# First attention's scores from rounded halves of q and k, both heads side by side in three products

## The reference

```
q = jnp.einsum('ahe,bce->bach', W_Q, x)      # x: layer norm of the input
k = jnp.einsum('ahe,bce->bach', W_K, x)
v = jnp.einsum('ahe,bce->bach', W_V, x)
scores = jnp.einsum('bach,baCh->bacC', k, q)
masked = jnp.where(causal, scores, -MASK_VAL)
attn = jax.nn.softmax(masked / sqrt(D_HEAD), axis=-1)
z = jnp.einsum('bacC,baCh->bach', attn, v)
out = jnp.einsum('aeh,bach->bce', W_O, z)
```

## Time and profile before

| | |
|---|---|
| median of 3 runs | 1166.75 us (1166.71 to 1169.32) |
| profiled execution, span | 1166.5 us |
| PE busy | 1131.5 us, 97% |
| DVE, ACT, POOL busy | 832.4, 709.4, 612.1 us |
| first attention | about 16 to 423 us |
| copies of k | 128 DMAs, 2.4 us to landing |

### The profile page before, as it was taken

How to read it: one execution, slowest core, us unless ns; L and a number is a source line. 1 busy time by engine, 2 the same in 40 slices (tenths; PEclk the granted TensorE clock), 3 DMA queues, 4 the chain that set the end, 5 groups by cost and what they waited for, 6 DMA issues and landing times.

```text
span 1166.5 us, 20317 instructions
## 1 busy us (share of the span) xinstructions
PE 1131.5 (97%) x6858; PEld 895.1 (77%) x6858; DVE 832.4 (71%) x2481; ACT 709.4 (61%) x1744; POOL 612.1 (52%) x641
## 2 busy tenths in 40 slices
PE   8899999999999999999989999999999999999997
PEld 6777877887788776577757887877878878777676
DVE  6788777878787556668887767768666777674553
ACT  3678777778776513543576756556666466575832
POOL 1455657565654311129786646538456465573330
PEclk9999999999999999999999999999999999999999
DMA  8124545554532501021040000300002100001010
GB/s 270 40 53 139 167 129 164 153 167 129 163 113 69 181 19 55 1 95 36 19 159 16 1 1 1 127 1 2 1 19 97 55 1 1 1 14 60 20 37 19
DMA packets 40549, 81.48 MB, mean 70 GB/s; under 512 B 5888, under 2 KB 18304, under 8 KB 39936
## 3 DMA queue, kind: packets, MB, share of 16 engines
q1 hardware_dynamic: 40448, 80.20, 22.1%
HBM read 41.04 MB, written 22.36 MB: 54 GB/s over the span
## 4 chain that ended last, share of the span: by engine, by line
PE 88%; DVE 5%; ACT 4%; issue 1%; POOL 1%; DMA 0%; SPq 0%; DVEq 0%; ACTq 0%; POOLq 0%
PE psum L1551 53%; PE psum L1649 6%; PE psum L1631 5%; PE psum L1781 5%; PE psum L1830 5%; PE psum L1815 4%; PE psum L1797 4%; PE psum L1763 2%; ACT probs L909 1%; DVE probs L1156 1%; PE psum L1558 1%; PE psum L1737 1%; PE psum L1843 1%; PE psum L1854 1%; POOL probs L751 1%
## 5 line engine op out<-in xcount | busy, mean ns | idle before, releaser
L751 POOL TENSOR_TENSOR probs<-probs,rden 128x128 f32<-128x128 f32 (+3 forms) x256 | 178.1, 728 | 79.1 <-DVE rden L1168 79.1
L909 ACT ACTIVATE probs<-probs,negmax 128x128 f32<-128x128 f32 (+3 forms) x256 | 140.7, 552 | 14.2 <-DVE negmax L1163 13.6
L993 ACT ACTIVATE lp<-lp,lneg,rn 128x256 f32<-128x256 f32 (+1 forms) x256 | 143.6, 568 | 9.0 <-DVE lneg L1385 8.9
L1156 DVE CUSTOM_DVE_ANT_0 probs<-psum,causal 128x512 f32<-128x512 f32 (+3 forms) x256 | 109.9, 485 | 15.3 <-PE psum L1551 14.8
L784 POOL TENSOR_TENSOR lp<-lp,lrden 128x128 f32<-128x128 f32 x64 | 25.7, 401 | 166.4 <-DVE lrden L1390 166.4
L796 POOL TENSOR_TENSOR rn<-ssm,neg_half 128x8 f32<-128x8 f32 x64 | 108.5, 1696 | 0.0
L1373 DVE CUSTOM_DVE_ANT_0 lp<-psum,local 128x256 f32<-128x256 f32 (+1 forms) x256 | 84.1, 385 | 19.5 <-PE psum L1781 19.5
L787 POOL TENSOR_TENSOR lp<-lp,lrden 128x768 f32<-128x768 f32 x64 | 94.0, 1468 | 0.0
L874 ACT ACTIVATE pT<-psum 128x512 f32<-128x512 f32 (+1 forms) x96 | 47.1, 518 | 66.5 <-PE psum L1631 66.2
L1631 PE MATMUL psum<-ident,probs 128*128 128x128 f32 x640 | 85.4, 273 | 1.2 <-POOL probs L751 1.2
L1551 PE MATMUL psum<-q,k_rest 128*128 128x256 f32 (+2 forms) x256 | 85.3, 344 | 1.1 <-DMA k<-k_round 0.6
(11 more groups left out here) (172 smaller groups left out, 3242.6 us busy)
## 6 DMA issues: line engine op xcount, KB each, us to landing
k<-k_round SPq DMA_DIRECT2D x128, 128.0 KB, 2.4
w_raw<-in_w_all SPq DMA_DIRECT2D x22, 380.0 KB, 4.0
w_scratch<-w_half SPq DMA_DIRECT2D x22, 380.0 KB, 4.2
w_scratch<-w_rest SPq DMA_DIRECT2D x22, 380.0 KB, 4.6
x<-in_x SPq DMA_DIRECT2D x8, 512.0 KB, 6.2
aw<-in_w_quads SPq DMA_DIRECT2D x4, 768.0 KB, 5.1
wqkv_lo<-w_scratch SPq DMA_DIRECT2D x6, 512.0 KB, 6.5
wqkv_hi<-w_scratch SPq DMA_DIRECT2D x6, 512.0 KB, 4.6
```

The source lines that it names most:

```text
L751: ins = pool.tensor_tensor(pr, pr, rden[:, u % 2, h, i:i + 1].broadcast_to([P, TRI[i]]), ALU.mult)
L909: ins = act.activation(pr, pr, ACT.Exp, bias=negmax[:, u % 2, h, i:i + 1], scale=ADH ** -0.5, accum_out=den[:, u % 2, h, i:i + 1])
L993: ins = act.activation(pr, pr, ACT.Exp, bias=lneg[:, u % 2, h, w:w + 1], scale=rn[:, m % 2, w, 0, 2 * j + h:2 * j + h + 1], accum_out=lden ...
L1156: ins = dve.tensor_tensor_reduce(probs[:, u % 2, h, TRI_AT[i]:TRI_AT[i + 1]], bank[:, at:at + TRI[i]], causal[:, S - TRI[i]:S], 1.0, -3e38 ...
```

## The change

Scores are now computed from four tiles of 128 partitions, both heads in each: kh, kl, qh, ql (rounded half and remainder of k and q). Three products make a head's scores, kl·qh, kh·ql and kh·qh, each with 64 rows of contraction; head 0's and head 1's follow each other into two different banks. The item s is cut by columns instead of heads: sA is the row tiles of 512 and 384 columns of both heads (banks 0 to 3), sB those of 256 (banks 0 and 1). k2, q2 and the copies of k are gone, and rounding and remainder are one instruction of 128 partitions each. Transposes get fixed banks 4, 5, 2, 3, 4, 5 and z bank 4. Scores run two units ahead of z, projections three, and a unit's 20 transposes stand in one block. The next quad's weights are rounded in the cycles for the quad's last unit. The later stages' cycles are unchanged; the entry list differs.

```diff
-        UNIT_PE = ("t0 s0@1 t1 t2 s1@1 pk@2 t3 t4 t5 pq@2 z pv@2")
-        UNIT_DVE = ("s0@1 aw2@-1 t0 t2 s1@1 r0@1 t4 pk@2 aw0 pq@2 aw1 r1@1 z")
-        UNIT_ACT = ("t1 e0@1 pk@2 part t3 t5 aw0 pq@2 aw1 e1@1 pv@2 aw2")
-        UNIT_POOL = ("f0@6 f1@6 part@6")
+        UNIT_PE = ("sA@2 z sB@2 pv@2 pk@3 pq@3 t0@1 t1@1 t2@1 t3@1 t4@1 t5@1")
+        UNIT_DVE = ("sA@2 r0@1 z sB@2 r1@1 aw2@2 pk@3 aw0@3 t0@1 pq@3 aw1@3 t2@1 t4@1")
+        UNIT_ACT = ("e0@1 e1@1 pv@2 aw2@2 pk@3 aw0@3 pq@3 aw1@3 t1@1 t3@1 part@1 t5@1")
+        UNIT_POOL = ("f0@1 f1@1 part@1")
...
-                sp.wait_ge(k_hi, u + 1)
-                for h in range(2):
-                    for half in range(2):
-                        sp.dma_start(k2[half * ADH:(half + 1) * ADH, h].bitcast(F32),
-                                     k_round[h * ADH:(h + 1) * ADH].bitcast(F32)).then_inc(k_both, 16)
...
-                copy(q2[0:ADH, 0, :], bank[0:ADH, :])
-                copy(q2[ADH:P, 1, :], bank[ADH:P, :]).then_inc(q_hi, 1)
+                copy(qh[:, :], bank[:, :]).then_inc(q_hi, 1)
...
-                dve.tensor_tensor(q2[ADH:P, 0, :], bank[0:ADH, :], q2[0:ADH, 0, :], ALU.subtract)
-                dve.tensor_tensor(q2[0:ADH, 1, :], bank[ADH:P, :], q2[ADH:P, 1, :], ALU.subtract)\
-                    .then_inc(read[use[0]], 1)
+                dve.tensor_tensor(ql[:, :], bank[:, :], qh[:, :], ALU.subtract).then_inc(read[use[0]], 1)
...
-                for k, blocks in enumerate(S_TILES):
-                    bank = wait_free(pe, plan["s", u, h, k])
+                for k in S_PARTS[part]:
+                    banks_of = [wait_free(pe, plan["s", u, h, k]) for h in range(2)]
                     at = 0
-                    for i in blocks:
+                    for i in S_TILES[k]:
                         n = max(TRI[i], LOC)
                         cols = slice(i * P, (i + 1) * P)
-                        ins = product(bank[:, at:at + n], [(k_rest[:, h, cols], q2[:, h, 0:n]),
-                                                           (k2[:, h, cols], q2[:, h, 0:n])])
+                        for term, (kt, qt) in enumerate(((kl, qh), (kh, ql), (kh, qh))):
+                            for h in range(2):
+                                rows = slice(h * ADH, (h + 1) * ADH)
+                                ins = mm(banks_of[h][:, at:at + n], kt[rows, cols], qt[rows, 0:n], start=term == 0,
+                                         stop=term == 2)
```

pv.0 has moved behind pk.0, the second sequence's transposes and pq.0. The start list now ends with the transposes of unit 1, and the cycle takes over from there:

```diff
-        START_PE = ("xT.0 pv.0 pk.0 pq.0 xT.1 pv.1 xT.2 s.0.0 s.0.1 pk.1 pq.1 pv.2 t.0.0 pv.3 s.1.0 "
...
+        START_PE = ("xT.0 pk.0 xT.1 pq.0 pv.0 sA.0 sB.0 pk.1 pq.1 pv.1 sA.1 xT.2 sB.1 pk.2 pq.2 t.0.0 t.0.2 "
+                    "t.0.1 t.0.3 t.0.4 t.0.5 pv.2 sA.2 z.0 pq.3 sB.2 xT.3 pk.3 t.1.0 t.1.1 t.1.2 t.1.3 t.1.4 "
+                    "t.1.5")
```

More of the change, by code:

```diff
@@ L170, in build @@
         aw = sbt(r1, "aw", [P, 3, E2, 2 * P])
[L171 to L173 removed]
+        kh = sbt(r1, "kh", [P, S], F32R)
+        kl = sbt(r1, "kl", [P, S], F32R)
+        qh = sbt(r1, "qh", [P, S], F32R)
+        ql = sbt(r1, "ql", [P, S], F32R)
+        between = sbt(r1, "between", [P, S])
         v = sbt(r1, "v", [P, 2, T, 2 * P])
@@ L439, in unit_items @@
                     items.append((what, n))
-                if what in ("s", "e", "r", "f", "t"):
+                if what in ("sA", "sB"):
+                    items.append((what, n))
+                if what in ("e", "r", "f", "t"):
                     items.append((what, n, i))
@@ L443, in unit_items @@
                     items.append((what, n - FIRST_PART))
-                if what == "aw" and j == QUNITS - 3 and c < QUADS - 1:
+                if what == "aw" and j == QUNITS - 1 and c < QUADS - 1:
                     items.append((what, c + 1, i))
@@ L488, in build @@
                 turn((what, at[0]), "p")
-            if what == "s":
-                for k in range(3):
-                    take((what, *at, k), k)
+            if what in S_PARTS:
+                for k in S_PARTS[what]:
+                    for h in range(2):
+                        take(("s", at[0], h, k), S_BANKS[k][h])
             if what == "t":
-                turn((what, *at), "e")
+                take((what, *at), T_BANKS[at[1]])
             if what == "z":
-                turn((what, *at), "e")
+                take((what, *at), Z_BANK)
             if what == "awo":
@@ L660, in _ @@
                 layer_wqkv_lo(0, c)
-            sp.wait_ge(k_both, K_DMAS * NU)
+            for h in range(2):
+                wait_full(sp, plan["s", NU - 1, h, 2])
             for b in range(B):
@@ new lines, in rest_of_k, with masked_scores @@
+                dve.tensor_tensor(kl[:, :], bank[:, :], kh[:, :], ALU.subtract).then_inc(read[use[0]], 1)
+            def masked_scores(u, part):
+                if u == 0 and part == "sA":
+                    dve.wait_ge(ld_causal, 16)
+                for k in S_PARTS[part]:
+                    for h in range(2):
+                        bank = wait_full(dve, plan["s", u, h, k])
+                        at = 0
+                        for i in S_TILES[k]:
+                            ins = dve.tensor_tensor_reduce(
+                                probs[:, u % 2, h, TRI_AT[i]:TRI_AT[i + 1]], bank[:, at:at + TRI[i]],
+                                causal[:, S - TRI[i]:S], 1.0, -3e38, ALU.add, ALU.max, rowmax[:, u % 2, h, i:i + 1])
+                            at += TRI[i]
+                        ins.then_inc(read[plan["s", u, h, k][0]], 1)
+                if part == "sA":
+                    return
+                for h in range(2):
+                    for k in range(3):
+                        wait_read(dve, plan["s", u, h, k])
+                    dve.tensor_scalar(negmax[:, u % 2, h, :], rowmax[:, u % 2, h, :], -ADH ** -0.5, None, ALU.mult)\
+                        .then_inc(s_neg, 1)
@@ L1471, in _ @@
                     rest_of_q(*at)
-                if what == "s":
-                    masked_scores(*at)
+                if what in S_PARTS:
+                    masked_scores(at[0], what)
                 if what == "r":
@@ L1557, in keep_running @@
                 for _ in range(n):
-                    mm(psum[0][:, :], k_rest[:, 0, 0:P], k_rest[:, 0, :], start=True, stop=True)
+                    mm(psum[0][:, :], kl[:, 0:P], kl[:, :], start=True, stop=True)
             def transposed_x(b):
@@ L1893, in _ @@
                     project_v(*at)
-                if what == "s":
-                    scores(*at)
+                if what in S_PARTS:
+                    scores(at[0], what)
                 if what == "t":
```

104 lines of the change are left out of this document (41 added, 63 removed), and 86 rows, old and new, of tables (CLOSE_DVE, ENTRY_ACT, ENTRY_DVE, ENTRY_PE).

## The result

| | before | after |
|---|---|---|
| median | 1168.03 us (4 runs, 1166.71 to 1171.31) | 1154.2 us (4 runs, 1153.98 to 1154.47) |
| span of the profiled execution | 1166.5 us | 1152.6 us |
| ratio after / before | | 0.987, 95% interval 0.985 to 0.990 |

The account below looks back on a forecast made before the run. PE's instruction list was taken as the limit (busy 97% of the span). About 5 us from the start, 6.8 from columns less mode changes, the rest from waits: 17.0 off 1166.5, plus 0.25, gives 1149.8 us, range 1141 to 1163.

Parts of the forecast that it names:

- Columns: Score products in each unit: three side-by-side pairs take 1.92 us instead of 2.56, 0.64 us less.
- Changes of mode: PE switching between split and full products: about 0.2 us each, four a unit instead of two, giving back 0.4 us.
- The unit: PE's steady cycle: 11.5 - 0.64 + 0.4 = 11.25 us, against 11.65 measured before with its waits.
- The margins: Room in three chains: ql before sA 0.3 us, POOL's probabilities before t3 0.6, copies before z 0.2; all hold.
- The start: First units: z.0 begins at 41.6 us instead of 47.15, and z.1 at 52.4.
- a rival for the start: New lists gain nothing at the start (lower clock, missed waits): 1155 to 1157 us, inside the forecast's range; no separate chance.
- The entry: After z.29: PE reaches t.30.3 after 7.3 us, probabilities at 9.3; z.30 at about 377.5 against 394.52.
- The later stages move forward as a whole: Stages after the entry keep their cycles and simply shift by the 17.0 us gained.
- What lies around the span: Median of the runs against the profiled span: 0.25 us above it.
- The sum: Whole kernel: span 1166.5 - 17.0 = 1149.5 us, median 1149.8.

Follow-up runs that it names:

- experiment 1: Changed kernel with both score products of a pair on partitions 0 to 63, head 1 using head 0's q and k: span 1209.0 us.
- experiment 4: Changed kernel, sB behind pv: span 1157.0 us; or sA and sB together ahead of z: median 1154.68; the latter with pv in bank 1: 1146.67.
- experiment 7: Changed kernel plus unneeded transposes in three PE waits (17, 15 and 26): median 1149.78 us, span 1147.7.
- experiment 2: Changed kernel with a row tile's score products ordered three of head 0, then three of head 1, instead of alternating: span 1152.8 us.
- experiment 2's second run: Changed kernel with all six products of head 0 in a score item first, then head 1's six, bank waits ahead of the first: span 1184.8 us.
- The runs of the kernel with fills and three changes: Changed kernel with sA and sB together ahead of z, pv in bank 1, and unneeded transposes in three PE waits: median 1144.25 us.
- the first version with three changes: Changed kernel with sA and sB together ahead of z, sB in banks 4 and 5, z in banks 6 and 7, adapted start: median 1154.68 us.

## Why the prediction was right, and where its terms were off

**Columns, right.** 3 × 0.64 a unit for both heads, side by side: measured pair for pair, and its opposite in experiment 1.

**Changes of mode, right.** 0.2 each, 0.4 a unit; 0.19 for one more and 0.20 for one fewer by experiment 4.

**The unit, right.** Forecast 11.25, measured 11.23 for an ordinary one. The three quad changes take 11.48, 0.25 more each, forecast 0.3. The whole stretch from z.1 to z.28 took 304.2 us against 303.8.

**The margins, right for the first, and each other one larger than said.** ql ends at 166.10 and sA starts at 166.45, 0.35 where 0.3 was said:

```profile
164.81 0.69 DVE L1158 COPY pT<-psum 128x512 f32<-128x512 f32 x1 [0.44 <-PE psum L1615]
165.42 0.68 DVE L1115 TENSOR_TENSOR ql<-psum,qh 128x512 fp32r<-128x512 f32 x1
166.02 1.01 DVE L1158 COPY pT<-psum 128x256 f32<-128x256 f32 x2
```

POOL is done at 164.37 for a t3 due at about 165.3, a margin of 0.9 where I said 0.6. The copies for z end at 167.51 (t5 on ACT) for a z at 167.88, 0.37 where I said 0.2. The table names no wait of PE between 60 and 370 us.

**The start, wrong by two terms.** z.0 was put at 41.6. Without a fall of the clock the same start lists bring it at 41.48 to 41.80, so the working was right in sum. With the fall, as in the changed kernel's profile, it is 43.13. The text had the lower clock only as a rival for the start, "waits I missed" among it, and it is what happened. The second term is z.0 to z.1, 12.0 us with these lists at either clock, not 10.8. The forecast had the end of t.1 9.4 us after z.0; in experiment 7's kernel it is 10.5 (41.48 to 52.01). Of this 1.1 us, 0.8 is one wait: PE is through with pk.3 by 48.6, but t.1.0 starts at 49.40: its bank held the transposed x of the last sequence, and DVE's remainder of that (xnT_lo) is late. I had looked at t.1's probabilities there and not at its bank. So of the 4.8 us that z.1 was to come earlier, 2.1 came (57.21 before, 55.15 after), and 3.8 with the clock kept up (53.45).

**The entry, right but for the clock.** Forecast 7.3 us to t.30.3, a wait of 2.0 for POOL and z.30 ten after z.29; measured a wait of 1.7, 1.0 more for the copies of pT, and z.30 10.1 after z.29. Behind it the clock fell in the changed kernel and did not in the one before:

```profile
378.51 1.31 PE L1615 MATMUL psum<-ident,probs 128*128 128x128 f32 x10 [1.69 <-POOL probs L735]
380.80 4.07 PE L1633 MATMUL psum<-pT,v 128*64 128x512 f32 x16 [0.98 <-DVE pT L1158]
```

z takes 4.07 us there, 2.37 in the earlier trace rows. That a new wait would put PE on the lower clock was in no term.

**"The later stages move forward as a whole", wrong by 1.8 us, to the good.** From z.31 to the end it is 744.1 instead of 745.9 us. The lead over the kernel before is 12.2 us at z.31, 12.6 at the first transposes of the windowed probabilities (576.39 before, 563.77 after) and 13.95 a few steps on, where it stays. In these steps PE waited 2.4 us for lqT and 2.9 for lmax before, 0.3 and 0.8 after; they fell by more than was gained, and why they fell was not tested.

**What lies around the span, wrong.** The forecast took the median as 0.25 above the profiled span, from one execution's span and other executions' times. An execution of the changed kernel took 1154.38 us for a span of 1152.6. The medians of both kernels are 1.5 to 1.6 above their profiled spans.

**The sum.** Of 4.4 us between forecast and median, 1.35 are that last term. The span is 3.1 longer than said: 1.5 at z.0 and 1.6 behind z.30, both the lower clock; 1.2 from z.0 to z.1; 0.6 in cycles and entry; less 1.8 later. With the clock kept up, experiment 7's span is 1147.7, below the forecast's 1149.5. The mechanism and its prices were right; that the 1.8 later covers the 1.8 lost from z.0 to the entry is luck.

## What to carry to other kernels

Operands that fill only half of TensorE's rows ran beside another set for the time of one product, and three such terms beat two over the full rows, 1.92 against 2.56 us a unit, as long as the visits are few: count 0.2 us for every change of mode, and check whose bank the saved time then waits for. A PE that is busy 98% of the span still loses time to single waits of 2 to 3 us, since the lower clock can cost another 1.4 to 1.7 us at each, and 2.9 where it lasted longer; products that nobody needs, inside the wait, take that back if they don't overrun it. And a chain with 0.35 us of room is not a chain without influence: 0.69 us more on it cost the whole gain.

## What was not expected of the hardware

PE starts products out of the program's order when they go to different halves of the rows: in experiment 2 the fourth product starts 0.01 us after the first, ahead of the second and third. It does so over a short distance only: in experiment 2's second run, with six of a head in a row, the seventh product passes three waiting ones and not four, and a unit is 1.1 us longer, 0.9 of it from the order. The Trainium skill (TensorE: Matmul & The Clock Gate, the mechanism of row and column tiling) says that matmuls start and end strictly in the order of the program; these timelines disagree for the start.

Also not expected: the same wait of 2.0 us at the start brings the half clock in some executions and not in others (0.88 in the window above, 1.00 in experiment 2's), so a kernel's time varies with it by 1.4 us at that place alone. The runs of the kernel with fills and three changes lie within 0.08 us of each other, those of the first version with three changes, with mean clocks from 0.993 to 0.999, are 5.7 apart.
